# Local attention of the layers: fp32 or split 16-bit probabilities, masks on GpSimd or TensorE, and the output projection one round later

## What is computed

```python
h = shift_token(x)                       # second half of the columns, one row later
q, k, v = split(h @ wqkv)                # 3 x 512 columns
q = l2norm(q) * qs;  k = l2norm(k) * ksc
q, k = rotary_xpos(q, k)
sim = einsum('bhwid,bhwjd->bhwij', bq, bk)      # own window and the one before
sim = where((i < j) | (i > j + WINDOW) | (j == -1), -max, sim)
o = softmax(sim) @ bv
x = x + o @ wo
h = shift_token(x)
h = (h - mu) / sqrt(var + 1e-5) * lg + lb
a, g = split(h @ w1 + b1)                # 2 x 682 columns
x = x + (a * gelu(g)) @ w2 + b2
```

## Time and profile before

| | us |
|---|---|
| median of 3 runs | 3973.07 (3972.77 to 3973.07) |
| profiled execution | 3974.68 |
| its span | 3972.9 |
| TensorE busy in it | 3510.6, mean granted clock 0.96 |
| VectorE, ScalarE, GpSimd busy | 2638.4, 2148.6, 1522.5 |

### The profile page before, as it was taken

How to read it: one execution, slowest core, us unless ns; L and a number is a source line. 1 busy time by engine, 2 the same in 40 slices (tenths; PEclk the granted TensorE clock), 3 DMA queues, 4 the chain that set the end, 5 groups by cost and what they waited for, 6 DMA issues and landing times.

```text
span 3972.9 us, 72434 instructions
## 1 busy us (share of the span) xinstructions
PE 3510.6 (88%) x26976; PEld 2099.6 (53%) x26976; DVE 2638.4 (66%) x4180; ACT 2148.6 (54%) x2585; POOL 1522.5 (38%) x1584
## 2 busy tenths in 40 slices
...
GB/s 56 48 60 54 58 55 57 56 56 57 45 82 6 14 21 19 18 34 19 21 18 18 34 19 42 20 50 19 27 24 24 34 35 25 24 27 31 37 19 35
DMA packets 149003, 139.02 MB, mean 35 GB/s; under 512 B 11132, under 2 KB 147376, under 8 KB 148912
## 3 DMA queue, kind: packets, MB, share of 16 engines
...
...
## 4 chain that ended last, share of the span: by engine, by line
issue 29%; POOL 21%; PE 15%; DVE 4%; ACT 2%; POOLq 0%; DMA 0%; SPq 0%; DVEq 0%; ACTq 0%
POOL f_u L1478 7%; POOL f_u L1483 5%; PE f_p L1104 3%; PE f_p L1123 3%; POOL f_hT L1494 3%; POOL f_Pl L1502 2%; PE f_p L1145 2%; PE f_p L1023 2%; POOL f_xb L1511 2%; PE f_p L1086 2%; POOL f_Pl L1504 1%; POOL f_qst L1488 1%; PE f_p L1090 1%; POOL f_mark_l L1499 1%; DVE f_negm L1360 1%
## 5 line engine op out<-in xcount | busy, mean ns | idle before, releaser
L654 DVE TENSOR_REDUCE m_negm<-m_p 128x2 f16<-128x1024 f32 x512 | 608.3, 1221 | 170.4 <-PE m_p L473 168.5
L576 ACT ACTIVATE m_Pr<-m_p 128x1024 f32<-128x1024 f32 x512 | 500.6, 1020 | 163.9 <-PE m_p L492 159.4
L1478 POOL TENSOR_TENSOR f_u<-f_u,f_bt 128x1024 f32<-128x1024 f32 x128 | 301.9, 2358 | 561.2 <-DVE f_bt L1332 561.2
L1104 PE MATMUL f_p<-f_vl,f_Pl 128*128 128x65 f32 x3584 | 426.1, 279 | 30.7 <-POOL f_Pl L1504 30.7
L1104 PEld LDWEIGHTS f_p<-f_vl,f_Pl 128*128 128x128 f32 x3584 | 416.0, 195 | 41.0 <-POOL f_Pl L1504 31.4
L1229 ACT ACTIVATE f_Pl<-f_p 128x896 f32<-128x896 f32 x256 | 220.5, 914 | 328.8 <-PE f_p L1090 221.6
L1494 POOL TENSOR_TENSOR f_hT<-f_gates,f_hT 128x512 f16<-128x512 f32 x192 | 223.8, 1166 | 396.5 <-ACT f_gates L1252 395.1
L501 PE MATMUL m_o<-m_Pr,m_vm 128*32 128x512 f32 x2048 | 341.6, 645 | 13.0 <-ACT m_Pr L576 13.0
L1023 PE MATMUL f_p<-f_wq_h,f_xT_h 128*128 128x512 f16 x768 | 295.8, 385 | 62.4 <-DVE f_mark_x L1318 45.1
L1244 ACT ACTIVATE f_gates<-f_p,f_bias 128x512 f32<-128x512 f32 x192 | 131.4, 684 | 344.8 <-PE f_p L1145 344.7
L1360 DVE TENSOR_REDUCE f_negm<-f_p 128x4 bf16<-128x1024 f32 x256 | 295.7, 1222 | 15.0 <-PE f_p L1056 15.0
...
## 6 DMA issues: line engine op xcount, KB each, us to landing
f_xs<-out SPq DMA_DIRECT2D x32, 512.0 KB, 4.8
f_xr<-out SPq DMA_DIRECT2D x32, 512.0 KB, 4.6
out<-f_xb SPq DMA_DIRECT2D x32, 512.0 KB, 3.3
m_xin<-in_L_attn_x SPq DMA_DIRECT2D x16, 512.0 KB, 4.1
out<-m_xn SPq DMA_DIRECT2D x16, 512.0 KB, 3.0
m_QT<-m_hi SPq DMA_DIRECT2D x128, 64.0 KB
m_KT<-m_hi SPq DMA_DIRECT2D x128, 64.0 KB
m_xr<-in_L_attn_x SPq DMA_DIRECT2D x16, 512.0 KB, 4.8
```

The costliest lines, as they stand in the source:

```text
L576: act.activation(Pr[kt % 2][:, 2 * u:2 * u + 2, :].rearrange("p h t -> p (h t)"), psum[w.slot("M2", g, kt, u)][:, :], ACT.Exp).then_inc(*w ...
L654: dve.tensor_reduce(negm[:, t, pr // 2, :, pr % 2], psum[w.slot("M1", h, u)][:, :].rearrange("p (a k) -> p a k", a=2), AX.X, ALU.max, nega ...
L1104: mm = pe.matmul(psum[w.slot("PV", hp)][:, e * T + t * (DH + 1):e * T + (t + 1) * (DH + 1)], Pl[h % 4][:, at * W:(at + 1) * W], vl[:, j, h ...
L1478: pool.tensor_tensor(u[t][:], u[t][:], bt[:], ALU.add).then_inc(*bt_used.up(I))
```

## The change

Attention: the exp is taken twice, once to fp16 in SBUF (`Pp[..][:, 0]`) and once in place, fp32, in the scores' own bank. VectorE (`p_lo`, step PL) subtracts the first from the second into an fp16 low part and frees the bank only then. v is split in the same way (step V on VectorE). A block of PV is three fp16 matmuls. The masks are added to the scores by TensorE in L2, and POOL's step L2 is gone. `bt` has two buffers and `hp_` three. The last W1 tile multiplies gates and values together with weights laid side by side (`wt`). SH moves from VectorE to GpSimd, as does the root of the layer norm (step LR; LN keeps the statistics and LA applies them). OT and WO become a group of their own, D, of item i - 2, a round after that item's PV and in the round of its N. `st_o`, where wo is loaded, moves to the buffers of P, and its load (WS) waits for the last PV of the layer before; it stands on SP at the end of the tail.

```diff
-        "PE": """C.V,0 C.V,1 C.V,2 C.V,3 A.XT C.ST,0 A.QK,0 C.ST,1 A.QK,1 C.ST,2 A.QK,2 C.ST,3 A.QK,3 F.W1,0 F.W1,1 C.L1,0 C.L1,1
-               F.W1,2 C.L1,2 C.L1,3 F.W1,3 F.W1,4 F.W1,5 C.LM F.W2,0 C.L2,0 F.W2,1 F.W2,2 C.L2,1 C.PV,0 C.L2,2 C.L2,3 C.PV,1 C.PV,2
-               C.OT,0 C.PV,3 N.XH C.OT,1 C.WO,0 C.WO,1 C.WO,2 C.WO,3""",
+        "PE": """C.V,0 C.V,1 C.V,2 C.V,3 A.XT C.ST,0 D.OT,0 D.OT,1 A.QK,0 C.ST,1 A.QK,1 C.ST,2 A.QK,2 C.ST,3 A.QK,3 D.WO,0 D.WO,1
+               C.L1,0 D.WO,2 D.WO,3 C.L1,1 F.W1,0 C.L1,2 F.W1,1 C.L1,3 F.W1,2 F.W1,3 C.LM F.W1,4 F.W1,5 C.L2,0 F.W2,0 F.W2,1 C.L2,1
+               C.PV,0 F.W2,2 C.L2,2 C.L2,3 N.XH C.PV,1 C.PV,2 C.PV,3""",
...
+        "ACT": """C.V,0 C.V,1 C.V,2 C.V,3 A.XT C.ST,0 D.OT,0 D.OT,1 A.QK,0 C.ST,1 A.QK,1 C.ST,2 A.QK,2 C.ST,3 A.QK,3 F.W1,0 F.W1,1
+               F.H1,0 F.W1,2 F.H1,1 C.LM F.W1,3 F.H1,2 F.W1,4 F.H1,3 F.W1,5 F.H1,4 C.L2,0 F.H1,5 C.L2,1 A.HI,0 C.L2,2 A.HI,1 N.XH
+               C.L2,3 A.HI,2 A.HI,3""",
+        "DVE": """C.V,0 C.V,1 C.V,2 C.V,3 A.XT D.OT,0 D.OT,1 D.WO,0 D.WO,1 A.QK,0 A.QK,1 A.QK,2 A.QK,3 C.L1,0 D.WO,2 D.WO,3 C.L1,1
+               F.W1,0 C.L1,2 F.W1,1 C.L1,3 C.LM F.W1,2 N.LN F.W1,3 F.W1,4 A.RN F.W1,5 F.ZB C.PL,0 F.W2,0 N.LA C.PL,1 F.W2,1 F.W2,2
+               C.PV,0 C.PL,2 N.XH C.PL,3 C.PV,1 C.PV,2 C.PV,3""",
+        "POOL": """A.QK,0 A.QK,1 A.QK,2 A.QK,3 F.H1,0 F.H1,1 F.H1,2 F.H1,3 F.H1,4 A.NM,0 N.LR F.H1,5 A.SQ,0 A.SH,0 A.NM,1 A.SQ,1 A.SH,1
+               A.NM,2 A.SQ,2 A.SH,2 A.NM,3 A.SQ,3 A.SH,3 N.LS""",
+        "SP": """A.XT N.LX F.W2,0 F.W2,1 F.W2,2 C.XR N.XH""",
...
-        vl = sb("vl", [P, NT, H, DH + 1], F32)
+        vl = sb("vl", [P, NT, H, 2 * DH + 1], F16)
-        Pall = sb("Pl", [P, 4, NK], F32)
+        Pall = sb("Ph", [P, 4, 2, NK], F16)
...
+                for e in range(2):
+                    for j in range(NT):
+                        pe.matmul(dst(e, j), identb[:], masks[:].rearrange("p a k -> p (a k)")[:, 0:min(2 * W, T - j * W)],
+                                  start=False, stop=False, skip_group_check=True)
...
-                            mm = pe.matmul(psum[w.slot("PV", hp)][:, e * T + t * (DH + 1):e * T + (t + 1) * (DH + 1)],
-                                           Pl[h % 4][:, at * W:(at + 1) * W], vl[:, j, h, :], start=(t == 0), stop=(j == t),
-                                           skip_group_check=True)
+                            pe.matmul(dst, p_hi, vl[:, j, h, 0:DH + 1], start=(t == 0), stop=False, skip_group_check=True)
+                            pe.matmul(dst[:, 0:DH], p_hi, vl[:, j, h, DH + 1:], start=False, stop=False, skip_group_check=True)
+                            mm = pe.matmul(dst, p_lo, vl[:, j, h, 0:DH + 1], start=False, stop=(j == t), skip_group_check=True)
...
-                    act.activation(Pl[h % 4][:], psum[w.slot("L2", h)][:, 0:NK], ACT.Exp, scale=1 / KBOOST)\
-                        .then_inc(*w.frees("L2", h))
+                    scores = psum[w.slot("L2", h)][:, 0:NK]
+                    act.activation(Pp[h % 4][:, 0, :], scores, ACT.Exp, scale=1 / KBOOST)
+                    act.activation(scores, scores, ACT.Exp, scale=1 / KBOOST).then_inc(*p_ready.up(I))
...
+            def p_lo(I, hp):
+                for h in (2 * hp, 2 * hp + 1):
+                    dve.wait_ge(*p_ready.at(I, h + 1))
+                    dve.tensor_tensor(Pp[h % 4][:, 1, :], psum[w.slot("L2", h)][:, 0:NK], Pp[h % 4][:, 0, :], ALU.subtract)\
+                        .then_inc(*w.frees("L2", h))
...
+            def la(I):
+                dve.wait_ge(*rstd_ready.at(I, 1))
...
+            def lr(I):
...
+                pool.wait_ge(*mv_ready.at(I, 1))
...
+            def ws(I):
+                if I.b > 0:
+                    hold(on_ready.at(all_of_layer(I.b), 0))
+                load(I, wo_loaded, st_o, wo[I.b].rearrange("(c p) n -> p c n", p=P))
```

More of the change, by code:

```diff
@@ L829, in layers_phase @@
     K = [Inst(f"K{layer}", 0, (lambda i, layer=layer: layer)) for layer in range(L)]
-    sections = [Section("queries", {engine: [("WQ", K[0])] for engine in ENGINES})]
+    sections = [Section("queries", {engine: [("WQ", K[0]), ("WS", K[0])] for engine in ENGINES})]
     for layer in range(L):
         more = layer > 0
-        r0 = weave(("first", layer), A=0, **(dict(N=-1, F=-2) if more else {}))
+        r0 = weave(("first", layer), A=0, **(dict(D=-1, N=-1, F=-2) if more else {}))
         r1 = weave(("second", layer), A=1, C=0, **(dict(F=-1) if more else {}))
-        r2 = weave(("third", layer), A=2, C=1, N=0)
-        if not more:
-            for engine in ("ACT", "DVE"):
-                with_steps(r0, engine, "start", ("WO_", K[0]))
-        with_steps(r0, "PE", "end", ("WO_", K[layer]))
+        r2 = weave(("third", layer), A=2, C=1, D=0, N=0)
+        for engine in ("ACT", "DVE"):
+            with_steps(r0, engine, "end" if more else "start", ("WO_", K[layer]))
+        with_steps(r1, "PE", "end", ("WO_", K[layer]))
         with_steps(r1, "SP", "end", ("WE", K[layer]))
```

166 lines of the change are left out of this document (92 added, 74 removed).

## The result

The changed kernel takes 4009.1 us (median of 4 runs, 4008.9 to 4010.0) against 3973.1 for the kernel before: the ratio is 1.0088, with a 95% interval of 1.0071 to 1.0106. It is slower by 36 us, where 3910, 63 us faster, was forecast. The profiled execution's span is 4008.2 us; that of before is 3972.9, and the two are compared from here on.

What follows compares the result with a forecast made beforehand. TensorE's matmul queue was taken as the bound, busy 79.07 of 81.85 us a steady round. Span 3972.9 - 47 (26 steady rounds) - 16 (irregular) = 3909.9, with 1.8 around the span and 1.6 off 3910; range 3840 to 3985.

Steps and rivals of the forecast that it cites:

- TensorE's queue: Steady round on TensorE: PV 5.8 us less, masks 3.5 more, joint W1 tile 1.3 less; net 3.6 us less matmul work.
- Rival C: PV steps on TensorE: weight loads set the pace, 77 ns a matmul, round 84.3 us, time 4019; chance 0.12.
- The order up to x1: Steady round from first V matmul: XT at 5.6 us, QK0 9.8, x1 written at 32, W1 until 49.25.
- The hole ahead of PV2: Round's end on TensorE: a ScalarE - VectorE - TensorE chain leaves holes of 0.3, 0.8 and 2.9 us.
- The wait costs nothing, with no slack left: Shift of x1, 14.3 us, delays LN; W1,3's product frees its bank at 49.15, L2,0 needs it at 49.25: no cost.
- rival D: Shift of x1: x1 comes 2 us later, L2,0 starts 2 us later, round 82.0 us, time 3962; chance 0.10.
- The clock: TensorE's clock falls after holes at the round's end, in half of the rounds, 0.85 us each.
- The irregular rounds: Ten rounds outside the steady ones, at the layers' starts and ends, gains and losses together: -16 us.
- the round late: From x1 to the next W1, 28.2 us before: D.OT, D.WO, then the shift in the open; 42.5, +14.5 us.
- The last steady round with tail 1: End of layer 1: -1.8 us for the steady round and -4.5 for tail 1.
- the second of layer 1: Second round of layer 1: OT and WO leave its end, L2 no longer waits behind HI,0 and GpSimd's masks; -10 us.
- E: Boundary rounds: no round gains, new holes grow to what is removed; 3973 + 10 to 20 us; chance 0.08.

Runs made afterwards that it cites:

- experiment 5: Changed kernel with residual addition earlier, shift of x1 in two transfers, and PV1 and L2,3's exps ahead of XH: 3884.2 us, ratio to before 0.9775.
- Experiment 2: Changed kernel with the shift of x1 issued as two transfers of 112 and 15 partitions: 3939.6 us, ratio to before 0.9915.
- experiment 4: Changed kernel with PV1 on TensorE, L2,3's exps on ScalarE and PL3 on VectorE each moved ahead of XH: 3973.5 us.
- experiment 1: Changed kernel with VectorE's residual addition (F.ZB, layer 1) moved from before C.PL,0 to before F.W1,0: 3977.7 us.
- experiment 12: Kernel of experiment 5 with VectorE's LN behind C.PL,0 and LA behind C.PL,1 in the two third rounds alone: 3878.4 us, ratio 0.9759.
- three repairs: The edits of experiment 1, Experiment 2 and experiment 4; all together on the changed kernel they measured 3884.2 us.

## Why the prediction was wrong, step by step

**TensorE's queue: right, and more favourable than forecast.** A PV step is 42 matmuls in 1.30 us, 31 ns each; I took 41, between bounds of 27 and 56. The masks are 0.77 us a pair, not 0.87. With the shorter W1 tile TensorE lost more work than the 3.6 us forecast: its busy time in a round at clock 1.00 fell from 79.07 to 73.67 us (experiment 5). Rival C, the loads as PV's pace, needed 62 ns and falls, and with it the rule of the Trainium skill quoted there: its 81 ns at 128 columns say nothing of 65 columns, which start every 31 ns.

**The order up to x1: right.** From the first V matmul on: XT at 5.66 us (forecast 5.6), QK0 at 10.0 (9.8), x1 written at 32.2 (32), last W1 at an end of 49.6 (49.25), no hole between WO and L1. The hole ahead of PV2 was forecast too, at 2.9 us, and is 3.03.

**"The wait costs nothing, with no slack left": the step that failed.** I took the transfer at the 14.3 us of one row of before and saw that each further us would be paid. It took 16.0, L2,0 started at 51.0 instead of 49.3, and the 1.7 us went through to PV2 (77.8 instead of 75.8). The 14.3 us ran from x1 to the end of a window that I had chosen, about where the last bytes moved. In after these moved at 15.3 us, at 19 GB/s instead of 20, and the way from there to VectorE's first statistics, 0.7 us, stood in no term. This is rival D's mechanism, in the transfer rather than in x1's time. Experiment 2 takes 70 us out by removing the whole wait; some 17 of these lie in the first round of layer 1 and at the end, where the forecast had a wait for the shift. A term whose slack is nil by one's own reckoning is no zero. I had also looked at the 10.7 us of one issue without asking why 0.26 MB take 14 us, though the DMA share of 0.07 in the same row is about one engine of 16.

**The clock: right in kind, too small in size.** I had it fall in half of the rounds, 0.85 us each on average. It fell in all 24 intervals; PV2 and PV3 took 0.9 to 1.6 us longer for it, and in layer 1 a second fall added some 1.5 us in 7 of 12. What the fall behind PV2 costs the whole round isn't shown. In experiment 4 it cost nothing, since XT waited for VectorE either way.

**ZB: the step that was missing.** The prediction says nothing on F.ZB ahead of C.PL,0. Its place costs 2.4 us in a mean steady round of layer 1, 31 us in experiment 1. On VectorE it is 1.2 us of its own and 1.2 for standing beside GpSimd's NM; in TensorE's queue it is a hole of 1.86 us and the clock's second fall behind it.

**The irregular rounds: sum -16 forecast** (its terms add up to -15.5). The first round of layer 0 came out near (+1.1 for +1.5), that of layer 1 better (+8.0 for +13). Of the end, the round late came out near, 43.6 us for 42.5 (TensorE from D.OT at 3935.76 to the last item's W1 at 3979.35), and the last one too (-1.1 for -1.5). The last steady round with tail 1 did not: it is 2.4 us longer, where 6.3 less was forecast. The second of layer 0 gained more than forecast. The third rounds and the second of layer 1 gained almost nothing. For the third, the step that was missing is the move of the bank's release from ScalarE to VectorE, whose queue there is full; experiment 12 took back 5.8 us of the 15.5 that the two third rounds missed by. The second of layer 1 lost its 7 us of projection and has holes of 4.56 us (ahead of the masks of L1) and 3.25 us (ahead of a PV) and a clock of 0.90 in their place; I didn't test that one.

**The rivals.** D was given 0.10 at 3962 and has the right mechanism for layer 0; E, also slower, says that the new holes grow to what is removed, which is what layer 0 shows (81.74 for 81.84). The time lies above the range because the steady rounds missed the forecast by 1.7 us in layer 0 and 4.1 in layer 1, 69 of the 98 us by which the differences of the table exceed the forecast ones; the shift, ZB and the clock, at nil or too small in the sum, all have the same sign. The order of experiment 4 is no such miss: its hole was in the forecast, and the edit is an order that I hadn't looked for. The rest is mainly the third rounds (15.5), the second of layer 1 (8.5) and the end (10).

**What each part is worth,** from the runs:

| kernel | us | rounds |
|---|---|---|
| before | 3973 | 81.84, 81.87 |
| before with masks on TensorE (7) | 4054 | 84.90, 84.92 |
| with late projection, joint W1 tile and the other moves as well, three repairs, 32-bit P (6) | 3927 | 80.89, 80.97 |
| the same with 16-bit P (5) | 3884 | 79.15, 79.15 |
| the same without the three repairs: the changed kernel | 4009 | 81.74, 84.12 |
